# Shared experts, first half: two groups by seven block products, weight sums through GpSimd's queue, one routed matrix split in the routed stage

## The chip, the cores and the metric

One core of one Trainium2 chip runs the whole program. The metric is the device time of an execution in microseconds (us). Three runs of the kernel before took 1921.5 to 1924.93 us, with a median of 1923.02.

## The reference, cut to what matters

Four layers, each added to its input, work on `x` of 2 x 2048 tokens with 512 features, in single precision. The third is a mixture of experts, and the change lies in it:

```python
for e in range(2):                       # shared experts, hidden width 1024 each
    h = silu(x @ s_w1[e].T) * (x @ s_w3[e].T)
    shared_out += h @ s_w2[e].T
s = sigmoid(concat(x, t_emb) @ W_router.T)   # top 2 of 8 experts per token
for e in range(8):                       # routed experts, hidden width 512
    h = gelu(x @ r_w1[e].T)
    routed_out += h @ r_w2[e].T * gates[:, e:e+1]
out = (shared_out / 2 + routed_out) / 4
```

Before it stand a gate with a Haar-like transform and a recurrent layer, behind it a leaky recurrent layer.

## The kernel before, in words

**Stages in order of time.** Recurrent layer (to about 268 us), `shared_part` with `part` 0 for the first four groups of 512 tokens (269.9 to 788), `routed_part` for the routed experts (to about 1158), `shared_part` with `part` 1 for the other four groups (to about 1663), leaky layer (to the end).

**An item.** The two shared experts together have 16 tiles of 128 hidden columns (`HID`). One item `n` is one tile of one group of 512 tokens; `gl, i = divmod(n, HID)`, so a part has 64 items in four groups 0 to 3. Every factor is kept as two half-precision parts (high and low), and a product is three products of parts: high by high, low by high, high by low. A *plain* item is `first(n)` (line 1334: two banks of 12 products of 512 columns) and `second(n)` (line 1405: 12 products of 512 columns into four banks that run over the whole group). Between them ScalarE takes silu of the first bank (L1610), VectorE multiplies by the second (L2083), ScalarE casts the high half (L1581) and VectorE subtracts for the low half (L1990).

**A seven-product item.** The two halves of `first` form a 2 x 2 block product, which can be done with seven block products of 256 columns (L1344, 42 products) in place of eight, from sums and differences of blocks of the weights and of `x`. Three weight sums of a tile (`ring_pair`, `ring_one`) are read back from the tensor `mixed`, a fourth (`s3`) is put over a quarter of the tile in the arena. The sums of `x` are made on VectorE (`raw_block`) and split like `x` (`split_block`, `low_block`). TensorE does `first_four(n)`, `second(n-2)`, `last_three(n)`; in between VectorE adds the block products (`middle_sums`, `last_sums`), ScalarE copies one and takes silu in two halves. Before, part 1 uses this for groups 1 to 3 and part 0 not at all.

**Weight sums.** Part 0 makes them, for part 1, in the items behind `MIX_AT`: SyncE loads 512 KB of a weight tile into the one buffer `mix` (L1161), VectorE adds four times (`mix_sums`, L1926 to L1931), ScalarE casts the high half into `mixed` (`mix_high`, L1547; it waits for the store of the sum before), VectorE makes the low half (`mix_low`, L1935), and SyncE stores 512 KB (L1165). Five of the sixteen stand in items 15 to 23, every second one, eleven in items 41 to 61.

**What else stands in part 0's items.** Weight tiles are split up to item 13 (`split_tile`). From item 2 to 25 the router looks at the tokens: of every three items two split a look of 512 tokens (`split_look`, L1541 and L1843, four blocks a look at two per item) and turn it by transposing DMAs, the third has the logits on TensorE (L1419) and the store of the look. Then come the routing steps (`route`), the row sums of the routed weights on VectorE (`row_sums`, L1717, 16 items), and the splitting of the 16 routed matrices (`split_matrix`, L1528 and L1710), eleven of which lie in the arena over tiles of shared weights and wait in group 3 until these have been used (`h_used`). `leave` adds a finished group to its residual (L2195). The order on each engine's queue is written out by hand, item by item; each engine works its queue in order. GpSimd issues only the gathers of token rows (L2167, L2245) here.

```python
act.wait_ge(mix_sum, MIXES * (t + 1))          # mix_high, ScalarE
if t:
    act.wait_ge(mix_stored, 16 * t)
nc.scalar.activation(mixed[:, :, 0, :], mix[:].rearrange("p (s n) -> p s n", s=MIXES), ACT.Copy, scale=scl[:, 1:2]).then_inc(mix_hi, 1)
```

Of the kernel before, what the change touches and what calls it, by code (L numbers as in the profile page):

```python
# [14 lines left out]
P = 128  # L15
# [844 lines left out]
QUARTER = PIECE // 2  # L860
MIXES = 4
MIX_AT = tuple(range(14, 24, 2)) + tuple(range(40, 62, 2))
# [6 lines left out]
def matrix_end(b):  # L869

    last = RBASE + (b + 1) * 2 * MATRIX - 1
    return last // (2 * TILE) if last < EBASE else None

# [47 lines left out]
def shared_part(nc, src, part, keep, x_in, x_out, dram):  # L921
# [13 lines left out]
    LOADED = HID if first_part else HID - 1  # L935
    load_tile = lambda q: hidden(q + HID - LOADED)

    with ExitStack() as ctx:
# [11 lines left out]
        if first_part:  # L950
            mix, mixed = sb("mix", [P, MIXES * QUARTER]), sb("mixed", [P, MIXES, 2, QUARTER], F16)
        else:
            v1, u2, ring_pair1 = sb("v1", [P, CW]), sb("u2", [P, CW]), sb("ring_pair1", [P, 4 * QUARTER], F16)
# [26 lines left out]
        chain, hop = sem("chain"), sem("hop")  # L980
        if first_part:
# [30 lines left out]
            mix_in, mix_sum, mix_hi, mix_lo, mix_stored = (sem(n) for n in ("mix_in", "mix_sum", "mix_hi", "mix_lo", "mix_stored"))  # L1012
# [7 lines left out]
        else:  # L1020
# [8 lines left out]
            s_in, s3_in = [sem("s_in0"), sem("s_in1")], [sem("s3_in0"), sem("s3_in1")]  # L1029
            x_first, y_first, x_second, y_second = (sem(n) for n in ("x_first", "y_first", "x_second", "y_second"))  # L1030
            v1_ready, u2_ready, w_ready, c22_ready, c_ready, silu2_ready = (sem(n) for n in ("v1_ready", "u2_ready", "w_ready", "c22_ready", "c_ready", "silu2_ready"))
            t_raw, lo_ready, lo_stored, lo_back = (sem(n) for n in ("t_raw", "lo_ready", "lo_stored", "lo_back"))
# [18 lines left out]
        ROUTE_STEPS = 8 + LISTS + 1  # L1051
# [3 lines left out]
        ROUTE_AT = look_at(LOOKS)  # L1055
        NORM_AT = ROUTE_AT + 1
        SCALE_AT = NORM_AT + NORMS_R
        order = [b for b in range(2 * EXPERTS) if matrix_end(b) is None] + [b for b in range(2 * EXPERTS) if matrix_end(b) is not None]
        E_AT = SCALE_AT + 3

        def split_at(j):

            last = matrix_end(order[j])
            return E_AT + j if last is None else (PART_GROUPS - 1) * HID + (last - 1) + 1

# [14 lines left out]
        plain = lambda n: first_part or n < HID  # L1080
# [15 lines left out]

        if not first_part:
            halves = {"b11": (0, 0), "b21": (0, 1), "b12": (1, 0), "b22": (1, 1)}

            def quarter_of(x, name):  # L1100
                c, k = halves[name]
                return x[:, c, k * KD // 2:(k + 1) * KD // 2, :]

            raw_t = {n: xold[:, i // 2, i % 2 * KD // 2:(i % 2 + 1) * KD // 2, :] for i, n in enumerate(("t1", "t3", "t2", "t4"))}
            X_ORDER = ("b11", "b21", "b22", "t1", "t3", "t2", "t4")

            def x_block(gl, name):


                slot_x, high, low = xres[slot(gl)], xh[slot(gl)], xl[slot(gl)]  # L1110
                if name in halves:
                    return [quarter_of(t, name) for t in (slot_x, high, low)]
                if name == "t1":
                    return [raw_t[name], quarter_of(high, "b12"), quarter_of(low, "b12")]
                more = extra[gl % 2][:, ("t2", "t3", "t4").index(name)]
                return [raw_t[name], more[:, 0], more[:, 1]]
# [3 lines left out]
        with nc.Block(no_gpsimd_drain=True) as block:  # L1120
            @block.sync
            def _(sp):
# [35 lines left out]
                def load_mix(t):  # L1158
                    if t:
                        sp.wait_ge(mix_lo, t)  # L1160
# [151 lines left out]
            def _(pe):  # L1312
# [185 lines left out]
                if not first_part:  # L1498
                    second(ITEMS - 2)
# [974 lines left out]
```

## Time and profile before

| | us |
|---|---|
| median of three runs | 1923.02 |
| the profiled execution | 1924.83 |
| its span, first to last instruction | 1923.2 |
| TensorE busy in the span | 1889.9 (98%) |
| VectorE / ScalarE / GpSimd busy | 1161.6 / 913.6 / 157.2 |
| `shared_part`, part 0 | 269.9 to 788 |

Rows of a timeline give the start in us from the span's start, the duration (of a merged run of like instructions), the engine (PE is TensorE's products, DVE VectorE, ACT ScalarE, POOL GpSimd, SPq SyncE's DMA issues), the line, what is written and read, and in brackets the idle time of the engine just before with what ended it. The duration of a product is its latency; products overlap, so a rate is read from starts.

### The profile page before, as it was taken

The numbers are of one execution on the slowest core, as the hardware profiler recorded it, in microseconds if no ns is written. First come the engines' busy times: TensorE is split into PE (matmuls) and PEld (weight loads), VectorE is DVE, ScalarE is ACT, GpSimd is POOL, SyncE is SP. The second block draws the span as 40 slices with busy tenths as digits, with TensorE's granted clock in tenths as the row PEclk, the third lists the DMA queues.
The fourth block names the chain that finished last, engine by engine and source line by source line (L and its number), as shares of the span: only waits on it lengthen the run. The fifth ranks groups of instructions, "written<-read, shape, count | busy, mean of one in ns | idle before, by whom it ended". The sixth has DMA issues, their size and how long they took to land. (4 is left out here: it accounts for less than half of the span.)

```text
span 1923.2 us, 46865 instructions
## 1 busy us (share of the span) xinstructions
PE 1889.9 (98%) x18676; PEld 1220.0 (63%) x18676; DVE 1161.6 (60%) x2541; ACT 913.6 (48%) x1939; POOL 157.2 (8%) x159
## 2 busy tenths in 40 slices
PE   8999989999999999999999999999999999999998
PEld 7999954444444434444444444457777777799997
DVE  6666646555688565412111115678877887688887
ACT  4444445424122344434333335534445554488886
POOL 0000000000000000122121102111111120000000
PEclk8999999999999999999999999999999999999999
DMA  7033337876453565799999967655554467233223
GB/s 309 14 131 131 132 139 190 228 210 196 144 176 121 197 201 182 166 258 204 225 217 198 208 142 240 188 165 167 147 169 138 138 163 245 75 112 90 47 47 58
DMA packets 307486, 312.94 MB, mean 163 GB/s; under 512 B 229416, under 2 KB 248494, under 8 KB 300399
## 3 DMA queue, kind: packets, MB, share of 16 engines
q1 hardware_dynamic: 294334, 267.01, 48.2%
q0 software_dynamic: 12960, 43.26, 9.6%
q8 instruction: 134, 2.20, 0.5%
q14 instruction: 58, 0.47, 0.1%
HBM read 190.93 MB, written 73.14 MB: 137 GB/s over the span
## 5 line engine op out<-in xcount | busy, mean ns | idle before, releaser
L1334 PE MATMUL sh_p<-xh,arena 128*128 128x512 f16 x1280 | 383.5, 381 | 7.4 <-ACT sh_gated L1610 4.8
L1405 PE MATMUL p<-sh_h_hi,arena 128*128 128x512 f16 x1024 | 304.6, 379 | 1.0 <-DVE sh_h_lo L1990 1.0
L1334 PE MATMUL sh_p<-xl,arena 128*128 128x512 f16 x640 | 244.1, 381 | 0.0
L2351 DVE SCALAR_TENSOR_TENSOR ro_hs<-ro_h,fac,ro_hs 128x512 f16<-128x512 f32 x71 | 53.4, 752 | 295.2 <-ACT ro_hs L2337 290.8
L1334 PEld LDWEIGHTS sh_p<-xh,arena 128*128 128x128 f16 x1280 | 125.7, 98 | 160.6 <-issue 5.9
L2294 PE MATMUL ro_py<-arena,ro_ht 128*128 x852 | 195.0, 379 | 0.0
L1405 PE MATMUL p<-sh_h_lo,arena 128*128 128x512 f16 x512 | 194.0, 379 | 0.0
L1581 ACT CAST sh_h_hi<-sh_gated 128x512 f16<-128x512 f32 x128 | 79.1, 618 | 234.4 <-DVE sh_gated L2083 207.7
L1405 PEld LDWEIGHTS p<-sh_h_hi,arena 128*128 128x128 f16 x1024 | 96.4, 98 | 106.7 <-DVE sh_h_lo L1990 1.7
L2294 PEld LDWEIGHTS ro_py<-arena,ro_ht 128*128 128x128 f16 x852 | 83.4, 98 | 100.5 <-issue 0.2
L2083 DVE SCALAR_TENSOR_TENSOR sh_gated<-sh_p,fac,sh_gated 128x512 f32<-128x512 f32 x80 | 59.9, 749 | 101.9 <-PE sh_p L1334 101.6
L1344 PE MATMUL sh_p<-xh,arena 128*128 128x256 f16 x672 | 118.1, 273 | 0.8 <-DVE sh_u L1969 0.4
L1990 DVE TENSOR_TENSOR sh_h_lo<-sh_gated,sh_h_hi 128x512 f16<-128x512 f32 x128 | 88.1, 688 | 47.5 <-ACT sh_h_hi L1581 47.2
L2333 ACT ACTIVATE ro_h<-ro_pf,fac 128x512 f32<-128x512 f32 x71 | 48.8, 687 | 137.0 <-PE ro_pf L2294 137.0
L1610 ACT ACTIVATE sh_gated<-sh_p,fac 128x512 f32<-128x512 f32 x80 | 54.5, 682 | 120.8 <-PE sh_p L1334 120.7
L1334 PEld LDWEIGHTS sh_p<-xl,arena 128*128 128x128 f16 x640 | 62.9, 98 | 76.5 <-issue 1.6
L2181 POOL DMA_INDIRECT arena<-routed_rows,slots x64 | 72.9, 1139 | 355.0 <-DVE sh_pair L1839 344.5
L381 PE MATMUL rnn_acc<-rnn_x_hi,rnn_wx_hi 128*128 128x256 f32 x336 | 98.9, 309 | 1.8 <-ACT rnn_wx_hi L510 1.8
L2294 PE MATMUL ro_pf<-arena,xres 128*128 x432 | 99.0, 379 | 1.3 <-PEq L1120 1.3
L551 ACT ACTIVATE rnn_h_hi<-rnn_acc,rnn_inv_scale 128x256 f16<-128x256 f32 x84 | 39.8, 474 | 125.2 <-PE rnn_acc L398 125.2
L1344 PE MATMUL sh_p<-arena 128*128 128x256 f16 x720 | 98.2, 273 | 0.6 <-DMA arena<-mixed 0.6
L381 PE MATMUL leaky_acc<-leaky_x_hi,leaky_wx_hi 128*128 128x256 f16 x352 | 96.1, 273 | 0.5 <-DVEq L680 0.5
(335 smaller groups left out, 3960.5 us busy)
## 6 DMA issues: line engine op xcount, KB each, us to landing
stage<-in_shared_w SPq DMA_DIRECT2D x29, 768.0 KB, 5.3
routed_rows<-xres SPq DMA_DIRECT2D x71, 256.0 KB, 2.6
stage<-in_norms_r SPq DMA_DIRECT2D x16, 1024.0 KB, 4.9
stage<-in_routed_w SPq DMA_DIRECT2D x16, 1024.0 KB, 6.4
stage<-in_norms SPq DMA_DIRECT2D x14, 1024.0 KB, 5.0
arena<-x SPq DMA_DIRECT2D x12, 1024.0 KB, 5.7
x<-xres SPq DMA_DIRECT2D x16, 512.0 KB, 2.6
x_rows<-arena SPq DMA_DIRECT2D x8, 1024.0 KB, 9.0
```

Source lines behind the costliest of these rows:

```text
L381: mm = nc.tensor.matmul(acc[p][:, m, :], w[:, k, cols], x[p][:, k, :], start=(not gate and by_ones(q) and m % 2 == 0 and k == 0 and x is x ...
L1334: mm = nc.tensor.matmul(p1[u % P1][:], arena[:, w:w + P], x[slot(gl)][:, :, k, :], start=(j == 0), stop=(j == 3 * KD - 1))
L1344: mm = nc.tensor.matmul(out, a, b, start=(start and k == 0 and a is w_hi and b is x_hi), stop=(k == KD // 2 - 1 and b is x_lo), skip_group ...
L1405: mm = nc.tensor.matmul(p2[m][:], arena[:, w:w + P], h[n % 2][:], start=(i == 0 and j == 0), stop=(i == HID - 1 and j == 2))
L1581: nc.scalar.copy(h_hi[n % 2][:], full_h[n % 2] if plain(n) else gated[:, 0:GW]).then_inc(hh_ready, 1)
L1610: nc.scalar.activation(sig[n % 2], p1[2 * n % P1][:], ACT.Silu, scale=fac[:, 0:1]).then_inc(silu_ready, 1)
L1990: nc.vector.tensor_tensor(h_lo[n % 2][:], full_h[n % 2] if plain(n) else gated[:, 0:GW], h_hi[n % 2][:], ALU.subtract).then_inc(h_ready, 1)
L2083: nc.vector.scalar_tensor_tensor(full_h[n % 2], p1[(2 * n + 1) % P1][:], fac[:, 6:7], sig[n % 2], ALU.mult, ALU.mult).then_inc(full_ready, 1)
L2181: nc.gpsimd.indirect_dma_start(y[number % 2], None, dram["y"], bass.IndirectOffsetOnAxis(ap=slots[:, c, t:t + 1], axis=0)).then_inc(y_in[n ...
L2294: mm = nc.tensor.matmul(out, a[:, lhs + k * P:lhs + (k + 1) * P], experts[:, bass.ds(e, 1), w0 + w + k * D:w0 + w + (k + 1) * D].rearrange ...
L2333: nc.scalar.activation(h[t % 2], pf[t % 2][:], ACT.Gelu, scale=fac[:, 2:3]).then_inc(g_done, 1)
L2351: nc.vector.scalar_tensor_tensor(hs[t % TURNS][:, D:2 * D], h[t % 2], fac[:, 3:4], hs[t % TURNS][:, 0:D], ALU.mult, ALU.subtract).then_inc ...
```

## The change

- Groups 2 and 3 of part 0 are done in seven-product items (`SEVEN` is the first such item: 32 in part 0, 16 in part 1). The code for it, part 1's before, is shared by both parts; the blocks of `x` for group 2 are made in items 23 to 30, for group 3 in items 39 to 46.
- All sixteen weight sums stand in items 12 to 27, one in each. Two buffers `mix` are loaded, one `mixed` is kept. GpSimd's queue issues loads and stores, the loads of `s3`, and in groups 2 and 3 the ring loads. The quarter of tile 0 that `s3` covers is stored at item 15 and brought back in the routed stage.
- Row sums of the routed weights go from VectorE's reduction to four activations with an accumulated output on ScalarE. The lists of routed rows take three VectorE operations an item where there were sixteen. `route` starts one item later and has one empty step.
- Fifteen of the routed matrices are split in group 3 (before: eleven there, five in items just ahead of and behind its start), the one with number 10 at the start of the routed stage. The two matrices of an expert change places.
- Three token rows are gathered ahead of the routed stage where there were four.

```diff
-MIX_AT = tuple(range(14, 24, 2)) + tuple(range(40, 62, 2))
+MIX_AT = tuple(range(11, 11 + HID))
+MATRIX_AT = {15: 0, 11: 1, 12: 2, 13: 5, 14: 9}
+LATE_MATRIX = 10
...
+    SEVEN = 2 * HID if first_part else HID
...
-        plain = lambda n: first_part or n < HID
+        plain = lambda n: n < SEVEN
...
-            mix, mixed = sb("mix", [P, MIXES * QUARTER]), sb("mixed", [P, MIXES, 2, QUARTER], F16)
+            mix = [sb("mix", [P, MIXES * QUARTER])[:], keep["spare"][:].bitcast(F32)]
+            mixed = sb("mixed", [P, MIXES, 2, QUARTER], F16)
...
-                    if first_part and n in MIX_AT:
-                        load_mix(MIX_AT.index(n))
+                    if first_part and n == KEPT_AT:
+                        sp.wait_ge(stage_done, LOADED)
+                        sp.dma_start(dram["a21"], mixed_place(arena, 0)).then_inc(kept_out, 16)
...
+                def row_sums(b):
+                    q = LOADED + b
+                    act.wait_ge(stage_in[q % 2], in_stage(q))
+                    if b == 0:
+                        act.wait_ge(stage_done, LOADED)
+                    for r in range(KD):
+                        part = stage[q % 2][:, r * D:(r + 1) * D]
+                        total = nc.scalar.activation(part, part, ACT.Abs, accum_out=keep["sums"][:, NORMS_S + b, r:r + 1])
+                    total.then_inc(stage_done, 1)
...
                     act.wait_ge(mix_sum, MIXES * (t + 1))
                     if t:
                         act.wait_ge(mix_stored, 16 * t)
-                    nc.scalar.activation(mixed[:, :, 0, :], mix[:].rearrange("p (s n) -> p s n", s=MIXES), ACT.Copy, scale=scl[:, 1:2]).then_inc(mix_hi, 1)
+                    nc.scalar.activation(mixed[:, :, 0, :], mix[t % 2].rearrange("p (s n) -> p s n", s=MIXES), ACT.Copy, scale=scl[:, 1:2]).then_inc(mix_hi, 1)
...
+                    elif r == 0:
+                        dve.wait_ge(x_loaded[slot(gl)], 16 * ((gl + 1) // 2))
+                        dve.wait_ge(xt_stored, 16 * LOOKS)
...
-                    if i == (0 if first_part else 1) and gl:
+                    if i == (0 if gl < SEVEN_GROUP else 1) and gl:
                         leave(gl - 1)
...
+                    def load_mix(t):
+                        if t >= 2:
+                            pool.wait_ge(mix_lo, t - 1)
+                        pool.dma_start(mix[t % 2], src["shared_w"][hidden(t)][:, 0:2 * PIECE]).then_inc(mix_in[t % 2], 16)
+
+                    def store_mix(t):
+                        pool.wait_ge(mix_lo, t + 1)
+                        pool.dma_start(dram["mixed"][hidden(t)], mixed_flat).then_inc(mix_stored, 16)
+
+                    def load_s3(i):
+                        pool.wait_ge(p1_filled, 2 * (SEVEN - HID + i) + 2)
+                        pool.wait_ge(mix_stored, 16 * (i + 1))
+                        if hidden(i) == 0:
+                            pool.wait_ge(kept_out, 16)
+                        pool.dma_start(mixed_place(arena, hidden(i)), dram["mixed"][hidden(i)][:, 4 * QUARTER:6 * QUARTER].rearrange("p (h n) -> p h n", h=2)
+                                       ).then_inc(s3_in[i // (HID // 2)], 16)
+
+                    def load_mixed(n):
+                        e, t = n - SEVEN, hidden(n % HID)
+                        if e >= 2:
+                            pool.wait_ge(y_second, e - 1)
+                        pool.dma_start(ring_pair[e % 2], dram["mixed"][t][:, 0:4 * QUARTER]).then_inc(s_in[e % 2], 16)
+                        pool.dma_start(ring_one[e % 2], dram["mixed"][t][:, 6 * QUARTER:8 * QUARTER]).then_inc(s_in[e % 2], 16)
+
+                    pool.wait_ge(p1_filled, 2 * MIX_AT[0])
+                    load_mix(0)
+                    load_mix(1)
+                    for t in range(HID):
+                        store_mix(t)
+                        if t + 2 < HID:
+                            load_mix(t + 2)
+                        if t >= S3_AFTER:
+                            load_s3(t - S3_AFTER)
...
-                for t in range(RING, SLOT_TILES):
-                    pool.wait_ge(xt_in[t % XT], 16 * ((t - RING) // XT + 1))
+                for t in range(RING - 1, SLOT_TILES):
+                    if t >= RING:
+                        pool.wait_ge(xt_in[t % XT], 16 * ((t - RING) // XT + 1))
...
+                act.wait_ge(*late_loaded)
+                for a in (late_at + MATRIX // 2, late_at):
+                    nc.scalar.activation(arena[:, a:a + MATRIX // 2], late_raw[:, a - late_at:a - late_at + MATRIX // 2], ACT.Copy, scale=scl[:, 5:6]).then_inc(late_hi, 1)
...
+                for half, a in enumerate((late_at + MATRIX // 2, late_at)):
+                    dve.wait_ge(late_hi, half + 1)
+                    nc.vector.scalar_tensor_tensor(arena[:, MATRIX + a:MATRIX + a + MATRIX // 2], late_raw[:, a - late_at:a - late_at + MATRIX // 2], scl[:, 5:6],
+                                                   arena[:, a:a + MATRIX // 2], ALU.mult, ALU.subtract).then_inc(late_lo, 1)
                 add_shared(nc, keep, 0, (PART_GROUPS - 1) % 2)
```

## Rows read from the trace of the kernel before

**Rows 1.** TensorE in order of time, group 0: start us, us, engine, line
```profile
297.48 0.59 PE L1405 MATMUL p<-sh_h_hi,arena 128*128 128x512 f16 x2
...
306.05 0.59 PE L1405 MATMUL p<-sh_h_hi,arena 128*128 128x512 f16 x2
...
313.82 0.59 PE L1405 MATMUL p<-sh_h_hi,arena 128*128 128x512 f16 x2
```

**Rows 2.** the same view, two seven-product items of the second half
```profile
1334.28 0.59 PE L1405 MATMUL p<-sh_h_hi,arena 128*128 128x512 f16 x2
...
1341.45 0.59 PE L1405 MATMUL p<-sh_h_hi,arena 128*128 128x512 f16 x2
```

**Rows 3.** order of time around 699 us, and one stretch's busy times
```profile
693.87 0.43 DVE L1926 TENSOR_TENSOR sh_mix<-sh_mix 128x256 f32<-128x256 f32 x1 [5.86 <-DMA sh_mix<-in_shared_w]
...
699.43 1.04 PE L1334 MATMUL sh_p<-xh,arena 128*128 128x512 f16 x2 [4.79 <-ACT sh_gated L1610]
...
core 0: us, PE busy (x) PEld busy (x) DVE busy (x) ACT busy (x) POOL busy (x), PEclk, DMA share, GB/s
...
697.00:703.60 6.60, 4.17 (x10) 1.50 (x11) 5.03 (x5) 3.59 (x5) 0.00 (x0) 0.50 0.20 71
```

**Rows 4.** order of time on VectorE and ScalarE, one weight sum in item 15
```profile
394.20 0.75 DVE L2083 SCALAR_TENSOR_TENSOR sh_gated<-sh_p,fac,sh_gated 128x512 f32<-128x512 f32 x1 [4.30 <-PE sh_p L1334]
...
396.24 0.42 DVE L1926 TENSOR_TENSOR sh_mix<-sh_mix 128x256 f32<-128x256 f32 x1
...
397.95 1.15 ACT L1547 ACTIVATE sh_mixed<-sh_mix,scl 128x1024 f16<-128x1024 f32 x1 [2.35 <-DVE sh_mix L1931]
...
401.07 1.28 DVE L1935 SCALAR_TENSOR_TENSOR sh_mixed<-sh_mix,scl,sh_mixed 128x1024 f16<-128x1024 f32 x1
```

**Rows 5.** DMA issues (count, KB each, median us to landing), and GpSimd's start
```profile
mixed<-sh_mixed SPq DMA_DIRECT2D x5, 512.0 KB, 6.7
...
mixed<-sh_mixed SPq DMA_DIRECT2D x11, 512.0 KB, 3.0
...
out<-leaky_hist POOLq DMA_DIRECT2D x15, 512.0 KB, 5.5
...
1323.73 0.69 DVE L1839 TENSOR_TENSOR sh_pair<-arena,sh_pair 128x512 f16<-128x512 f32 x1 [1.03 <-ACT sh_pair L1649]
...
1324.69 1.75 POOL L2181 DMA_INDIRECT arena<-routed_rows,slots  x1 [14.69 <-DVE sh_pair L1839]
```

**Rows 6.** busy times by stretch (columns as in rows 3): look stage, second half
```profile
380.00:475.00 95.00, 95.00 (x555) 44.76 (x553) 50.15 (x82) 33.52 (x50) 0.00 (x0) 1.00 0.71 208
...
1278.00:1380.00 102.00, 100.65 (x745) 72.06 (x744) 85.30 (x158) 40.95 (x77) 14.80 (x14) 1.00 0.50 148
```

**Rows 7.** order of time on VectorE, and ScalarE's groups from 380 to 475
```profile
785.83 2.48 DVE L1710 SCALAR_TENSOR_TENSOR arena<-stage,scl,arena 128x1024 f16<-128x1024 f32 x2 [1.64 <-ACT arena L1528]
...
L1541 ACT ACTIVATE arena<-arena,scl 128x512 f16<-128x512 f32 x16 | 10.6, 710 | 2.1 <-DMA arena<-x 2.1
...
1339.44 0.68 DVE L1983 TENSOR_TENSOR sh_gated<-sh_p,sh_u 128x512 f32<-128x512 f32 x1
...
1342.91 0.68 DVE L1990 TENSOR_TENSOR sh_h_lo<-sh_gated,sh_h_hi 128x512 f16<-128x512 f32 x1
```

**Rows 8.** order of time on TensorE, second half; who waited for whom there
```profile
1280.82 0.59 PE L1405 MATMUL p<-sh_h_hi,arena 128*128 128x512 f16 x2
...
1319.93 0.59 PE L1405 MATMUL p<-sh_h_hi,arena 128*128 128x512 f16 x2
...
PE p L1405 <- DVE sh_h_lo L1990: 1.0, 1, 1.0
```

**Rows 9.** order of time at the start of the routed stage
```profile
789.29 0.95 POOL L2245 DMA_INDIRECT xh<-x_rows,token_of  x1 [132.71 <-POOLq L1120]
...
789.54 5.35 PE L2294 MATMUL ro_pf<-arena,xres 128*128 x24 [1.33 <-PEq L1120]
...
793.40 1.23 SPq L2254 DMA_TRANSPOSE xres<-xh  x1
```

More of the change, by code:

```diff
@@ L1054, in shared_part @@
         look_at = lambda a: 2 + 3 * a
-        ROUTE_AT = look_at(LOOKS)
+        ROUTE_AT = look_at(LOOKS) + 1
         NORM_AT = ROUTE_AT + 1
         SCALE_AT = NORM_AT + NORMS_R
-        order = [b for b in range(2 * EXPERTS) if matrix_end(b) is None] + [b for b in range(2 * EXPERTS) if matrix_end(b) is not None]
-        E_AT = SCALE_AT + 3
+        matrix_at = {b: (PART_GROUPS - 1) * HID + (MATRIX_AT[b] if matrix_end(b) is None else matrix_end(b) + (1 if matrix_end(b) < HID - 2 else 2)) for b in range(2 * EXPERTS)}
+        order = sorted(matrix_at, key=lambda b: matrix_at[b])
+        assert order[-1] == LATE_MATRIX and SCALE_AT + 3 < matrix_at[order[0]]
         def split_at(j):
-            last = matrix_end(order[j])
-            return E_AT + j if last is None else (PART_GROUPS - 1) * HID + (last - 1) + 1
+            return matrix_at[order[j]]
         def stage_load(q):
@@ L1257, in _ @@
                         load_x(1)
-                    if i == (1 if first_part else 2) and gl:
+                    if i == (1 if gl < SEVEN_GROUP else 2) and gl:
                         store_x(gl - 1)
@@ L1495, in _ @@
                         last_three(n)
-                    elif n and (first_part or n < HID - 1):
+                    elif n and n < SEVEN - 1:
                         second(n - 1)
-                if not first_part:
-                    second(ITEMS - 2)
+                second(ITEMS - 2)
                 second(ITEMS - 1)
@@ L1622, in _ @@
                         split_tile(n + AHEAD)
[L1623 removed]
+                    if i in BLOCK_AT and in_sevens(gl + 1):
                         split_block(gl + 1, BLOCK_AT.index(i))
@@ L2106, in _ @@
                         mix_sums(MIX_AT.index(n - 1))
-                    if not first_part and gl + 1 < PART_GROUPS:
+                    if in_sevens(gl + 1):
                         for r in range(len(RAW_AT)):
@@ L2168, in _ @@
                                                      ).then_inc(keep["rows_in"][t], 16)
+                    for n in range((PART_GROUPS - 1) * HID + 2, ITEMS):
+                        load_mixed(n)
                     keep["spent"] = spent
+                    late = LOADED + NORMS_R + 2 * EXPERTS - 1
+                    keep["late_raw"] = stage[late % 2], (stage_in[late % 2], in_stage(late))
                 else:
@@ L2234, in routed_part @@
         rows_in = keep["rows_in"]
+        late_raw, late_loaded = keep["late_raw"]
+        used.append(late_loaded[0])
+        late_at = RBASE + LATE_MATRIX * 2 * MATRIX
+        late_hi, late_lo, kept_in = sem("late_hi"), sem("late_lo"), sem("kept_in")
+        assert LATE_MATRIX % 2 == 0 and late_raw is keep["stage"][1]
         stage_in, x_loaded, xh_ready, xl_ready = sem("stage_in"), sem("x_loaded"), sem("xh_ready"), sem("xl_ready")
```

250 lines of the change are left out of this document (143 added, 107 removed).

## The prediction, made before the change was run

> **What bounds the kernel now.** The busy times by engine put TensorE at 98% of the span, so the question of every stage is whether TensorE gets less to do and whether it is then still fed. I read four views. First, TensorE's order of time in the plain items [rows 1]: the second product of an item begins every 7.77 us (306.05 to 313.82), and 8.57 us where the router's logits lie between (297.48 to 306.05, so 0.80 for them). Second, the same in the seven-product items of the other half [rows 2]: 7.18 us apart. Third, the one place in the first half where TensorE starves [rows 3]: at 693.87 VectorE had waited 5.86 us for the 512 KB load of a weight sum, and behind the cast of that sum in ScalarE's queue the activation that frees TensorE's bank came late: 4.79 us idle at 699.43. From 697.0 to 703.6 the granted clock is 0.50, the 1.2 GHz level, at which 4.2 us of products (699.43 to 703.6) do the work of 2.1. So this stall costs 4.8 + 2.1 = 6.9 us. Fourth, the chain of one weight sum inside an item [rows 4], which decides what follows.
>
> **What the change takes away.** 32 items (groups 2 and 3) go from 7.77 to 7.18: 32 x 0.59 = 19.1 us, all on TensorE and so on the path. The sums leave group 3, and with them the load that was late: 6.9 us. Together 26.0.
>
> **Part 1: sixteen weight sums in sixteen consecutive items (12 to 27).** Before they stood in every second item. Per item the chain on VectorE is: gate product, wait for ScalarE's high half, low half, 2.04 us (394.20 to 396.24); four sums, 1.71 (to 397.95); then ScalarE's cast of the sum, two blocks of the router's look on both engines, and the low cast, 4.40 (397.95 to 402.35) [rows 4]. That is 8.15 us in an item with look blocks. In the one item of three that has the logits instead, the two casts alone stand there, 1.15 + 1.28 = 2.43, so 6.2. Three items: 22.5 of VectorE's time against 3 x 7.77 + 0.80 = 24.1 of TensorE's. It fits, with 1.6 us to spare. Some lateness is allowed: VectorE has an item's low half 2.1 us after the item's first products, and TensorE uses it after the second product of the item before and the first products of the next, 7.77 us after them, so 5.6 us of room. Items 12 and 13, which still split a weight tile, use about half of that up.
>
> There is a second loop, which the spacing of two items hid before: `mixed` is one buffer, and ScalarE's cast of sum t waits (`mix_stored`) until the store of sum t-1 has landed. So from one low cast to the next there pass GpSimd's start, the landing L, and 4.40 (or 2.43). GpSimd starts an issue 0.27 us after VectorE's end (1323.73 + 0.69 to 1324.69) [rows 5]. Three items: 3 x (0.27 + L) + 2 x 4.40 + 2.43 = 3 L + 12.0, equal to TensorE's 24.1 at L = 4.0. Each us of L above that costs 3 us in three items, so 14 in items 12 to 25, less some 2 us of the lateness still allowed. The queue behind the wait is ScalarE's whole item: look blocks, the next activation, the next high half; TensorE waits for the last two.
>
> L is not in the trace. Bounds: 3.0, SyncE's 512 KB store of the same buffer in the quieter items after 580; and 6.7, the same store in items 14 to 23 [rows 5], where it queued behind SyncE's own 1 MB look loads. GpSimd's only direct store of 512 KB lands in 5.5 [rows 5], in a stretch with little else, but it adds into memory (`accum_op` at line 302), which this one does not. The engines are 71% busy in the stretch (380 to 475) [rows 6], and seven more sums there add 1 MB each to its 19.8 MB. I take L = 4.5, between SyncE's quiet store and GpSimd's adding one: 14 x 0.5 - 2 = 5 us, and 1 more for item 16, whose four residual additions stand in the same queue, and item 26, where the first raw block waits for the last look's store. **6 us**; ends 0 (L up to 4.1) and 14 x 2.7 - 2 = 36.
>
> The Trainium skill, page "DMA: Bandwidth & Descriptors", section "Anatomy of one DMA — SWDGE (gpsimd) path", gives a DMA of GpSimd's queue as 2.0 us plus its bytes over 436e3, so 3.2 for 512 KB. By that the store loop never closes and this part costs nothing; by the rows above it costs 6.
>
> **Part 2: the seven-product groups.** TensorE waits per item for VectorE's three middle sums. In the other half these groups ran with VectorE busy 85.3 of 102 us and TensorE 100.65 [rows 6]. From the last sums to the low half is 4.15 us (1339.44 to 1343.59), one routed matrix adds 2.48 [rows 7]: 6.6 of 7.18 in group 3. The matrices that lie over shared weights wait for `h_used`, 5.2 us into the item, so VectorE ends some 1.7 us into the next; the middle sums have 2.3 us of room there, and the next matrix waits for `h_used` anyway, so it doesn't add up. At the group's second item the residual additions (four, 2.7 us) come on top: 1 us, ends 0 and 2. Entry: in the other half the first five items took 39.1 us (1280.82 to 1319.93) for 35.9 [rows 8], 3.2 too long; part of that is that half's own work, so 2, ends 0 and 4. Exit: the last low half comes 1.0 us late there [rows 8], and the first half has the same tail: 1.0. The pair of ring loads moves to GpSimd's queue; issued when an item ends, they have 7.8 us, and the landings in rows 5 are below that: 0.
>
> **Part 3: row sums on ScalarE.** Four activations per item for VectorE's reduction, items 28 to 43. Not shown with an accumulator; the plain one of that size is 0.71 [rows 7], so 2.8 per item. ScalarE was busy 41 of 102 us, 2.9 per item, in the other half [rows 6]: 5.7 of 7.18, hidden by TensorE: 0. At twice the price 8.6, 1.4 too much in twelve items: 17 at the upper end. Nothing below zero, since VectorE's reductions were hidden.
>
> **Part 4: the routed stage's start.** One row gather moves behind the barrier. Before, the gather issued at 789.29 let SyncE start its transpose at 793.40 [rows 9], 4.1 later; a transposed tile is used about as long again after that, so at 797.5 or a little more. The fourth tile's product was due after three others of 2.67 (5.35 for two, from 789.54), at 797.5: 0.6, ends 0 and 3. The late matrix (2.2 on ScalarE, 2.48 on VectorE) goes before the first residual additions and is covered by the first four products, 10.7 us: 0.
>
> **The sum.** -26.0 + 6 + 1 + 2 + 1 + 0.6 = -15.4. The profiled execution is 1924.83 outside and 1923.2 inside; it lies 1.8 above the median. 1923.0 - 15.4 = 1907.6, about 1908.
>
> **Rivals.** *The store lands early (L up to 4).* Part 1 costs 0 to 1. For it: SyncE's 3.0. Against: GpSimd's 5.5. Time 1901 to 1903. This is also what the skill's fit would give.
> *The store loop rules (slower).* Place: ScalarE's cast in items 12 to 25. Price: 14 us per us of L. It takes back the whole remaining 21.4 at L = 5.7 and turns slower (by 0.2%, 3.8 us) at L = 5.9; at 6.4 it costs 32 and the time is 1933. For it: 6.7 in this very stretch and 5.5 on this very queue. Against: the 6.7 contains a wait in SyncE's queue that GpSimd's does not have. A clock drop like that of rows 3 would add to it.
> *ScalarE is the bound in items 32 to 43* (row sums at twice the price): 1908 + 17 = 1925, no change.
> *The change doesn't do what it says*: if TensorE is not the bound in groups 2 and 3, items stay at 7.77 and 19 us are missing: 1927. Rows 6 speak against it.
>
> **How the numbers follow.** A measurement of this kernel can tell 0.2%, 3.8 us, from no change. Chances: forecast (L 4.1 to 5.3) 0.45; early store 0.24; store loop with L above 5.6 0.18; ScalarE or seven-product groups bound 0.13. Faster: the first two, and 0.04 from milder forms of the others, 0.73. Same: 0.12, where gains and stalls cancel. Slower: 0.15. Range: 1900 (early store and a free entry) to 1925 (L = 5.7); what is left out is the slower end and a little below. The likeliest case alone has 1902 to 1917.
>
> **What would show it.** Right: 7.18 us between second products in groups 2 and 3; no idle of TensorE by ScalarE near item 60; in items 14 to 25 short stalls by the activation or the low half, ScalarE's cast idle "by DMA mixed". The store's median landing is the number to read. Wrong: stalls in group 3 by the matrix's cast or by ring loads, TensorE waiting in items 28 to 43 for ScalarE, or a long first gap in the routed stage.

## The result, and the profile after

The change made the kernel slightly slower: 1927.26 us (median of 20 runs, 1921.99 to 1934.37) against 1923.11 (median of 20, 1921.5 to 1926.49), a ratio of 1.0021 with a 95% interval of 1.0015 to 1.0027. Forecast were 1908 and faster; the range ended at 1925. The profiled execution is the longest of the twenty (1934.37, span 1932.6), 7 us above the median, so its stalls are larger than those of a usual execution.

The table cuts the span at starts that the traces show: second(11) and second(29) are the first products on the second weights of items 11 and 29 (what is ahead of second(11) differs by some 1 us), then come the first and the last routed product. Each row is one profiled execution.

| kernel | second(11) to second(29) | to the first routed product | routed stage |
|---|---|---|---|
| before | 145.7 | 274.1 | 368.0 |
| forecast for after | 151.7 | 252.1 | 368.6 |
| after | 167.0 | 254.5 | 375.3 |

The middle column came nearly as forecast. The groups by seven products run at 7.18 us an item, as in [rows 2], and where group 3 had stalled [rows 3] it no longer does. TensorE in order of time, after, two items of group 3, those between which the old stall lay:

```profile
705.08 0.59 PE L1429 MATMUL p<-sh_h_hi,arena 128*128 128x512 f16 x2
...
712.26 0.59 PE L1429 MATMUL p<-sh_h_hi,arena 128*128 128x512 f16 x2
```

The loss is in the other two columns. First the items of the weight sums. Who waited for whom in items 11 to 30 (us in total, times, longest):

```profile
ACT sh_mixed L1580 <- DMA mixed<-sh_mixed: 47.9, 12, 7.3
...
PE sh_px L1443 <- DVE arena L1874: 16.7, 5, 5.9
...
PE p L1429 <- DVE sh_h_lo L2025: 0.3, 1, 0.3
```

TensorE waits 16.7 us in five places, all at the router's logits (L1443) and all for the low blocks of a look, and next to nothing for activations or low halves. The order of time on all engines over two sums, after, shows where the lateness comes from:

```profile
416.71 0.37 SPq L1219 DMA_DIRECT2D x_rows<-arena  x1
...
420.07 0.54 POOL L2204 DMA_DIRECT2D mixed<-sh_mixed  x1 [10.15 <-DVE sh_mixed L1966]
...
426.79 1.15 ACT L1580 ACTIVATE sh_mixed<-spare,scl 128x1024 f16<-128x1024 f32 x1 [5.70 <-DMA mixed<-sh_mixed]
...
431.49 0.56 POOL L2204 DMA_DIRECT2D mixed<-sh_mixed  x1 [9.65 <-DVE sh_mixed L1966]
...
436.32 1.15 ACT L1580 ACTIVATE sh_mixed<-sh_mix,scl 128x1024 f16<-128x1024 f32 x1 [3.81 <-DMA mixed<-sh_mixed]
437.37 1.32 ACT L1574 ACTIVATE arena<-arena,scl 128x512 f16<-128x512 f32 x2
438.11 1.41 DVE L1874 SCALAR_TENSOR_TENSOR arena<-arena,scl 128x512 f16<-128x512 f32 x2 [3.29 <-ACT arena L1574]
...
439.58 1.02 PE L1443 MATMUL sh_px<-router_both,arena 128*128 128x16 f16 x32 [5.93 <-DVE arena L1874]
...
441.01 0.56 POOL L2204 DMA_DIRECT2D mixed<-sh_mixed  x1 [7.73 <-DVE sh_mixed L1966]
```

A store goes out at 420.07, ScalarE's next cast can start at 426.79; the next pair is 431.49 and 436.32. The two look blocks stand behind that cast on both engines, and TensorE, which works its queue in order, stands at the logits meanwhile. In or right behind three of the five stalls (4.2, 5.9 and 3.3 us) the granted clock falls to 0.50, the 1.2 GHz level; at the two shorter ones (2.3 and 1.0 us) it does not. Busy times by stretch, after (the first three rows are these places, the fourth is the routed start, the last covers the sums):

```profile
core 0: us, PE busy (x) PEld busy (x) DVE busy (x) ACT busy (x) POOL busy (x), PEclk, DMA share, GB/s
436.00:442.80 6.80, 3.22 (x38) 1.74 (x39) 4.01 (x6) 3.56 (x5) 1.79 (x3) 0.50 0.65 165
405.30:412.10 6.80, 4.67 (x42) 2.19 (x42) 3.96 (x5) 2.43 (x5) 1.06 (x2) 0.50 0.78 191
...
494.00:497.50 3.50, 3.50 (x31) 1.57 (x29) 2.78 (x6) 1.24 (x2) 1.79 (x3) 0.51 0.85 91
...
801.20:808.10 6.90, 5.46 (x13) 2.02 (x14) 0.00 (x0) 0.12 (x1) 2.83 (x3) 0.51 1.07 234
...
379.00:519.00 140.00, 125.61 (x699) 57.55 (x700) 82.25 (x141) 50.54 (x68) 23.44 (x40) 0.94 0.88 250
```

So of the 21.4 us that this stretch grew (second(11) at 368.71 and second(29) at 535.73, for 369.81 and 515.46), 17.0 are waits. The other 4.4 are products at the 1.2 GHz level, less some 0.9 us of the routing's products that moved out of the stretch: the 4.67, 3.22 and 3.50 us of products in the first three rows do the work of half that.

Second, the start of the routed stage, after, in order of time:

```profile
790.64 2.03 POOL L2339 DMA_INDIRECT xl<-x_rows,token_of  x1 [22.08 <-issue]
...
795.58 1.24 SPq L2350 DMA_TRANSPOSE stage<-xl  x1
...
802.64 5.30 PE L2393 MATMUL ro_pf<-arena,stage 128*128 x12 [4.49 <-DMA stage<-xl]
```

Row 3's gather, now behind the barrier, lets its transpose go out at 795.58, where the kernel before could issue that of row 4 at 793.40 [rows 9]. The product on the transposed tile starts 7.1 us later, TensorE idles 4.49 before it and then runs at 1.2 GHz (the fourth row above): the stage is 7.3 us longer than before, where 0.6 was forecast. There is no other wait of TensorE in it.

### The profile page after: what moved, and what is told of

It is laid out like the page before. It is cut to its first block and busy times, and to the rows that moved or that the text cites. A ratio compares the mean times of both kernels' runs of the same rounds, so it can differ in the third digit from the quotient of the medians.

```text
span 1932.6 us, 48465 instructions
## 1 busy us (share of the span) xinstructions
PE 1878.6 (97%) x19252; PEld 1276.1 (66%) x19252; DVE 1186.3 (61%) x2563; ACT 975.4 (50%) x2137; POOL 220.4 (11%) x271
## 5 line engine op out<-in xcount | busy, mean ns | idle before, releaser
L1358 PE MATMUL sh_p<-xh,arena 128*128 128x512 f16 x768 | 229.6, 381 | 2.6 <-PEq L2331 1.6
L1368 PE MATMUL sh_p<-xh,arena 128*128 128x256 f16 x928 | 163.5, 273 | 2.0 <-DVE arena L2004 0.7
L1614 ACT CAST sh_h_hi<-sh_gated 128x512 f16<-128x512 f32 x128 | 79.1, 618 | 157.0 <-DVE sh_gated L2118 112.8
L1358 PE MATMUL sh_p<-xl,arena 128*128 128x512 f16 x384 | 146.0, 380 | 0.0
L1358 PEld LDWEIGHTS sh_p<-xh,arena 128*128 128x128 f16 x768 | 75.2, 98 | 94.2 <-issue 4.1
L1368 PE MATMUL sh_p<-xl,arena 128*128 128x256 f16 x464 | 126.5, 273 | 0.0
L1368 PE MATMUL sh_p<-arena 128*128 128x256 f16 x912 | 124.4, 273 | 0.4 <-DMA arena<-mixed 0.4
L1608 ACT ACTIVATE sh_gated<-sh_gated,fac 128x256 f32<-128x256 f32 x80 | 40.6, 508 | 156.9 <-DVE sh_gated L2018 156.9
L1368 PEld LDWEIGHTS sh_p<-xh,arena 128*128 128x128 f16 x928 | 90.0, 98 | 32.2 <-DVE sh_u L2004 1.9
L2393 PE MATMUL ro_pf<-arena,stage 128*128 x420 | 98.9, 386 | 4.5 <-DMA stage<-xl 4.5
```

What stands on the lines that cost most here:

```text
L1358: mm = nc.tensor.matmul(p1[u % P1][:], arena[:, w:w + P], x[slot(gl)][:, :, k, :], start=(j == 0), stop=(j == 3 * KD - 1))
L1368: mm = nc.tensor.matmul(out, a, b, start=(start and k == 0 and a is w_hi and b is x_hi), stop=(k == KD // 2 - 1 and b is x_lo), skip_group ...
L1608: nc.scalar.activation(gated[:, CW:2 * CW], gated[:, CW:2 * CW], ACT.Silu, scale=fac[:, 0:1]).then_inc(silu2_ready, 1)
L1614: nc.scalar.copy(h_hi[n % 2][:], full_h[n % 2] if plain(n) else gated[:, 0:GW]).then_inc(hh_ready, 1)
L2393: mm = nc.tensor.matmul(out, a[:, lhs + k * P:lhs + (k + 1) * P], experts[:, bass.ds(e, 1), w0 + w + k * D:w0 + w + (k + 1) * D].rearrange ...
```

## The experiments

The theories: A, the look's blocks come late to the logits, where TensorE has no room for lateness; B, the store loop itself is too slow for one sum an item; C, VectorE's and ScalarE's own work is too long; D, there are more transfers than the engines can carry. All runs are timed beside the same kernel before; ratios are to it. The table gives the three stretches of each profiled execution. These are single executions of kernels whose times scatter by several us (the change's by 12), so small differences between them show nothing.

| run | median us | ratio (95%) | second(11) to (29) | to routed | routed |
|---|---|---|---|---|---|
| e1 | 1913.1 | 0.9945 (0.9932 to 0.9958) | 154.4 | 253.4 | 371.9 |
| e2 | 1939.0 | 1.0078 (1.0065 to 1.0091) | 174.1 | 255.6 | 372.5 |
| e3, e3b | 1917.5 | 0.9966 (0.9954 to 0.9978) | 154.6 | 253.9 | 370.3 |
| e4 | 1928.1 | 1.0019 (1.0010 to 1.0027) | 162.7 | 253.5 | 374.8 |
| e5 | 1921.3 | 0.9987 (0.9978 to 0.9997) | 157.0 | 253.7 | 372.3 |
| e6 | 1933.9 | 1.0048 (1.0034 to 1.0062) | 167.8 | 256.4 | 376.1 |
| e7 | 1924.7 | 1.0004 (0.9995 to 1.0013) | 164.3 | 253.6 | 372.5 |
| e9 | 1927.5 | 1.0018 (1.0009 to 1.0027) | 163.8 | 254.8 | 371.8 |
| e10 | 1939.9 | 1.0073 (1.0059 to 1.0087) | 163.7 | 273.9 | 368.2 |
| e11 | 1919.2 | 0.9981 (0.9965 to 0.9997) | | | |
| e12 | 1919.4 | 0.9979 (0.9971 to 0.9988) | 146.2 | 267.5 | 369.4 |
| e13 | 1910.2 | 0.9927 (0.9914 to 0.9940) | 148.3 | 253.9 | 369.0 |
| e14 | 1909.0 | 0.9927 (0.9914 to 0.9940) | 149.8 | 253.3 | 369.1 |
| e15 | 1913.2 | 0.9940 (0.9923 to 0.9957) | 152.8 | 254.1 | 368.0 |

### What stalls the logits: e1, e2, e3

The edits, in short:

```
e1, ScalarE's item:
-  mix_high(...)                  ahead of split_look
+  mix_high(...)                  behind split_look
e2, TensorE's item:
-  first(n); logits(a); second(n - 1)
+  first(n); second(n - 1); logits(a)     (scores one item later)
e3, buffers:
-  act.wait_ge(mix_stored, 16 * t)
+  act.wait_ge(mix_stored[buf(t)], 16 * uses(t))   two buffers in turn
```

Expected of e1:

> Edit: in ScalarE's item the cast of the weight sum stands behind the two look blocks instead of ahead of them; nothing else. Theory A (the look blocks, queued behind a cast that waits for the store of the sum before, reach the logits late; TensorE takes the logits right after the item's first products, so there is no room): the waits of TensorE for the look's low blocks (16.7 us in five places in the profiled execution) and the 1.2 GHz stretches behind them go; 12 to 18 us below 1927, so 1909 to 1915. Theory B (the store loop is too slow for one sum an item, whatever stands behind it): the loop gets shorter too, by the look blocks, so also most of it. Theory C (VectorE's and ScalarE's work in these items is too long in itself, without any wait for the store): the work is the same, 1927, and the waits move to other operands.

Expected of e2:

> Edit: TensorE's logits stand behind the second product of the same item instead of ahead of it (about 2.6 us later, and no product of this item behind them), VectorE's reading of the scores and the last sigmoid one item later; the weight sums, their cast, the wait for the store and the order on ScalarE and VectorE are otherwise as in the changed kernel. Theory A: a look that is 2.6 us late costs nothing now and one that is 6 us late costs some 3, so at least 8 of the 17 us go, with the 1.2 GHz stretches: 1911 to 1918. Theory B: the lateness itself remains and grows from item to item; TensorE waits for the activation or the low half of the next items instead: 1923 to 1929.

Expected of e3:

> Edit: the split sums go into two buffers in turn (the second in the free part of the scratch), so the cast of sum t waits for the store of sum t-2; orders and transfers are as in the changed kernel. Theories A and B (the wait for the store is the source of the lateness): ScalarE's waits for the store (47.9 us in twelve places) go, and with them 12 to 18 us: 1909 to 1915. Theory C (the engines' own work is too long): 1925 to 1929. Theory D (the transfers of the sums crowd out the look's own transfers): 1925 to 1929, since the traffic is the same.

e1 gave 14 us, as forecast, and e3 10, some 2 short of its range, without any work taken away, so theory C falls, and D with it as a full account (the transfers were the same). The waits of e1 in items 11 to 30, where those of the change were 47.9 and 16.7:

```profile
ACT sh_mixed L1580 <- DMA mixed<-sh_mixed: 28.4, 10, 5.0
...
PE sh_px L1443 <- DVE arena L1874: 5.6, 5, 3.6
```

e2 went wrong for both theories: it became 12 us slower. Its waits in the same items:

```profile
ACT sh_mixed L1580 <- DMA mixed<-sh_mixed: 56.2, 12, 9.9
...
PE sh_px L1443 <- DVE arena L1874: 11.7, 5, 3.8
...
PE sh_p L1358 <- ACT sh_gated L1643: 6.2, 3, 4.4
```

With more room at the logits the waits there shrink from 16.7 to 11.7, but ScalarE's waits for the store grow, and TensorE now waits for its activation as well. So the room at the logits is not the cause; it is where the lateness comes due. Theory B fits the waits of all three: the store loop is too slow for its three items, and what TensorE does not wait for in one place it waits for in the next. It does not give e2's time (1923 to 1929 expected, 1939 measured): why e2 lost still more, 7 us in this stretch, is open. The logits also free the look's buffers later there; whether that is it was not tried.

The same kernel ran once more for its trace. Expected of e3b:

> The kernel with two buffers for the split sums once more, for its trace: where its 10 us over a free run went. If the wait for the store was all: no waits of ScalarE for the store and waits of TensorE at the logits below 3 us in all. If ScalarE's order is a cost of its own (the look behind a cast that waits for VectorE's sums): 5 to 8 us of waits at the logits remain, released by the look's low blocks. If the look's load is late, ScalarE's idle time names it (8 us once).

Who waited in items 11 to 30, e3b:

```profile
PE sh_px L1449 <- DVE arena L1880: 6.3, 3, 2.7
...
ACT arena L1580 <- DMA arena<-x: 2.9, 1, 2.9
```

With two buffers ScalarE's cast never waited for a store in these items; 6.3 us at the logits stayed, the second case of the text ahead: the look still stands behind a cast that waits for VectorE's sums. Once the look's own load was late, by 2.9.

### Is it the amount of traffic? e5, e9, e10

In these items the transfer engines were 88% busy (the last row of the busy times), so the amount itself was the next suspect.

```
e5, SyncE, on top of e1:
-  turn_look(a, k) x2; load_look(a + 1)
+  load_look(a + 1); turn_look(a, k) x2
e9, on the change alone:
-  pool.dma_start(mix[t % 2], src["shared_w"][hidden(t)][:, 0:2 * PIECE])
+  w = 2 * PIECE if t < 2 else QUARTER
+  pool.dma_start(mix[t % 2][:, 0:w], src["shared_w"][hidden(t)][:, 0:w])
e10, on the kernel before, GpSimd:
+  for n in ten items of 12 to 26: two loads of 512 KB into free scratch
```

Expected of e5:

> Edit: on top of the cast behind the look (1913), SyncE issues the load of the next look ahead of the four transposes of this one instead of behind them. In the kernel with the cast behind the look alone, ScalarE waited 8.9 us for the last look's load (issued at 462.98, behind transposes that took SyncE's queue 9.0 us for five), and the logits after it cost 13.69 and 10.06 us for two items of 8.57 and 7.77. If SyncE's order makes the load late: those 7 us go, 1905 to 1908. If the load is late because the transfer engines are full (the load itself 8.5 us): it lands late all the same, 1911 to 1914.

Expected of e9:

> Edit on the changed kernel (1927) alone: from the third weight sum on, GpSimd loads only a quarter of the raw columns (128 KB for 512); every instruction, order, wait and store stays, and the sums are of older columns (left out: three quarters of the raw values, so the weights of groups 2 and 3 are other numbers). Theory of the transfer engines (items 12 to 27 ask for 35 MB, which at the 250 to 276 GB/s seen takes 127 to 140 us, where TensorE needs 121; everything that waits for a transfer is late by turns): 5.5 MB less bring the stretch to 29.5 MB and some 110 us, the stores land near 4 us, the waits at the logits shrink below 6 us: 1911 to 1916. Theory of order (the look behind the cast and the store loop are too long by themselves): stores still land after 4.6 to 5.1, 1923 to 1927.

Expected of e10:

> Edit on the kernel before: twenty more loads of 512 KB on GpSimd's queue into free scratch, two in each of ten items between 12 and 26, that nothing uses and only VectorE's first routing step waits for, long after; 10.5 MB more in the stretch, near what the change moves there. Theory of the transfer engines: although no sum was added, the stretch gets longer; the look's load, its transposes and its stores are late and TensorE waits at the logits: 3 to 8 us slower, 1927 to 1932. Theory of order: traffic alone costs nothing, 1923 to 1925.

e9 left the time where it was (1927.5). The transfers shrank, from 32.2 MB to 28.8 in the same 130 us, the stalls hardly did. The DMA view of 380 to 510 us, e9 (the last row: count, KB each, median us from issue to landing):

```profile
DMA packets 26988, 28.79 MB, mean 221 GB/s; under 512 B 19849, under 2 KB 20105, under 8 KB 26725
...
mixed<-sh_mixed POOLq DMA_DIRECT2D x14, 512.0 KB, 4.0
```

And who waited in items 11 to 30, e9:

```profile
ACT sh_mixed L1580 <- DMA mixed<-sh_mixed: 45.4, 12, 7.1
...
PE sh_px L1443 <- DVE arena L1874: 13.6, 5, 5.7
```

The median landing is 4.0 us, yet ScalarE waits for stores almost as long as in the change (45.4 for 47.9), and TensorE 13.6 for 16.7. The median landing fell as the theory of the transfer engines had it; the time and the waits came out as the theory of order had them. The reason is in the single stores. From a store's issue to the next cast that waited for it, three in a row: after 6.7, 4.8, 4.2 and 6.3, 3.9, 4.5; e9 7.2, 4.2, 4.0 and 7.9, 3.9, 4.0. One in three is long, and in the change it is always the one issued within a few us of SyncE's 1 MB store of the look's rows (416.71 and 420.07 above; also 387.39 and 389.40, 448.96 and 447.94, 476.76 and 474.78). That this store is what holds it up is read from the times; a kernel without it was not tried.

e5 fits neither of its cases: it became 8 us slower than e1, 7 above the upper range. With the look's load ahead of the transposes, ScalarE waited once 9.8 us for the transposes that free the look's buffer, and for the sums' stores up to 7.9; a transfer that is moved up moves others back. The waits of e5 in the same items:

```profile
ACT sh_mixed L1580 <- DMA mixed<-sh_mixed: 40.7, 11, 7.9
...
ACT arena L1574 <- DMA arena<-arena: 9.8, 1, 9.8
```

e10 shows that traffic can stall this stretch too, but it is not clean, and at 1939.9 it is slower than either case had it: of its 13 us at the logits and routing, half follows from the wait that was added for the extra loads. Its waits in the same items:

```profile
DVE arena L1880 <- DMA arena<-in_shared_w: 11.7, 1, 11.7
...
PE sh_px L1422 <- DVE arena L1846: 6.5, 1, 6.5
PE sh_px L1480 <- DVE arena L1884: 6.4, 1, 6.4
```

The first wait is VectorE's for the extra loads, and the 6.4 at L1480 follow from it. The 6.5 at L1422 come from traffic, but through the order again. Order of time, e10:

```profile
450.62 0.42 DVE L1930 TENSOR_TENSOR sh_mix<-sh_mix 128x256 f32<-128x256 f32 x1 [2.62 <-DMA sh_mix<-in_shared_w]
...
452.33 1.15 ACT L1550 ACTIVATE sh_mixed<-sh_mix,scl 128x1024 f16<-128x1024 f32 x1 [5.06 <-DVE sh_mix L1935]
453.39 1.32 ACT L1544 ACTIVATE arena<-arena,scl 128x512 f16<-128x512 f32 x2
```

The load of a weight sum, issued at 440.49, landed after 10.1 us; its cast waited on ScalarE, and the look's blocks stood behind that cast, as in the old stall of [rows 3] the activation did.

### The start of the routed stage: e4, e6, e7

```
e4: group 3 keeps its two running sums elsewhere from item 6 of the group on
+  row 3 gathered in group 3, ahead of the barrier
e6, on top of e4:
+  pool.wait_ge(xt_in[3], 16)     ahead of the gather of row 4
e7, on top of e4, ScalarE and VectorE:
-  late matrix in halves of 1024 columns
+  the 512 columns under row 3's transposed tile first, then 1536
```

Expected of e4:

> Edit: the two running sums of group 3 move, from its seventh item on, out of the place of gathered row 3 into the free half of the other residual buffer, and row 3 is gathered in that group, ahead of the barrier, as in the kernel before. The split of the late matrix stays behind the barrier. If the late gather holds up the routed stage (its transpose issued at 795.5, with three other gathers in flight, and landed 7 us later): the 4.5 us idle of TensorE at 802.6 and the 1.2 GHz stretch go, 5 to 7 us: 1920 to 1922. If it is the late matrix (its split frees the place of the third and fourth transposed tile): at most 2 us, 1925 to 1927.

Expected of e6:

> Edit: on top of the early gather of row 3 (1928), GpSimd's gathers of rows 4 and later wait until the transpose of row 3 has landed. Theory of contention (in the profile the transpose of row 3 was issued while gathers were in flight and landed 7 to 8 us later, where two transposes alone took 3): row 3's tile is there about 3.5 us after its issue, the 1.9 us of idle at the fourth product go, row 4 comes later but in time; the routed stage starts 3 to 5 us sooner: 1923 to 1925. If the gathers are not what holds it, rows 4 to 6 come later for nothing: 1929 to 1932.

Expected of e7:

> Edit: on top of the early gather of row 3 (1928), the late matrix is split in two unequal pieces, the quarter that lies in the place of row 3's transposed tile first (512 columns), then the rest, so that this tile's transpose waits for 1.2 us of ScalarE and VectorE instead of 2.4 and goes out right behind that of row 2, ahead of the gathers, as in the kernel before. Theory: the wait of 1.3 us for the late matrix let the gathers of rows 4 and 5 overtake the transpose; without it the start is the one before, 5 to 6 us better: 1921 to 1923. If the gathers slow it anyway, or GpSimd's first gather (2.03 us instead of 0.95) does: 1926 to 1928.

e4 alone gave nothing (1928.1, above both of its ranges). Row 3 was there in time, but its transpose now waited 1.3 us for the late matrix, and it went out among the gathers of rows 4 to 6. Order of time, e4:

```profile
785.85 2.03 POOL L2350 DMA_INDIRECT xh<-x_rows,token_of  x1 [22.07 <-issue]
...
787.10 1.23 SPq L2361 DMA_TRANSPOSE stage<-xl  x1
...
795.23 2.76 PE L2404 MATMUL ro_pf<-arena,stage 128*128 x12 [1.88 <-DMA stage<-xl]
...
800.88 1.60 PE L2404 MATMUL ro_py<-arena,ro_ht 128*128 x4 [2.89 <-DMA ro_ht<-ro_hs]
```

Issued at 787.10, it landed 8.0 us later. The longer wait, 2.89, is for the first transposed tile of the second step: its transpose stands in SyncE's queue behind that of row 4, and the gather of row 4 took 9.0 us to land. With the last quarter first (e7) the fourth product had no idle, and the median fell by 3.4, between the two ranges, though its one profiled execution shows a later wait of 2.6 us for a transposed tile of the second step. Holding the gathers back (e6) did what its first case said to row 3's tile, which landed after 4.4 us instead of 8.0 and was not waited for, but it made row 4 late: TensorE waited 5.7 us for the first transposed tile of the second step, again behind the transpose of row 4, and the time rose to 1933.9. In the five profiles with e4 and e7 together (e7, e12 to e15) the stage is 368.0 to 372.5, four of them within 1.5 us of the kernel before; in the six with the change's start (after, e1, e2, e3b, e5, e9) 370.3 to 375.3. So the start costs some 4 us, up to 7.3. With row 3 early and the late matrix still behind the barrier it costs as much (e4), partly by a late gather; the late row alone was not tried, and the shares of the two are open.

### Putting it together: e11 to e15

```
e11 = e1 and  MIX_AT: items 12 to 29, without 18 and 24
e12 = e11 with e3, e4 and e7
e13 = e1, e3, e4, e7, sums in items 12 to 27 as in the change
e14 = e1, e4, e7 (one buffer), sums in items 12 to 27
e15 = e13 with sums in items 12 to 28, without 21
```

Expected of e11:

> Edit: the cast behind the look (1913) and the sixteen sums over eighteen items (12 to 29, none in 18 and 24) instead of sixteen. Theory of the transfer engines: 1 MB less in two of the windows of three items, so 2 to 5 us: 1908 to 1911. If only the order mattered: 1912 to 1914. Risk: the last sum ends two items later, and the first ring loads of group 2 come behind its store: up to 4 us back, seen as TensorE waiting for ring tiles at item 32.

Expected of e12:

> Edit: cast behind the look, sums over eighteen items, two buffers for the split sums, row 3 gathered early, and the late matrix's last quarter first. If the parts add up (cast 14, two buffers some of the 28 us that ScalarE still waits for stores, spread 2 to 5, start of the routed stage 3): 1902 to 1907. If the transfer engines set the stretch whatever the order: the two buffers add nothing, 1906 to 1910.

Expected of e13:

> Edit: cast behind the look, two buffers for the split sums, row 3 early and the last quarter first, the sums in sixteen items in a row again (12 to 27). With the sums over eighteen items this had no stall in items 12 to 27, but 11.7 us at item 32, where the first ring tiles came late (1919). If the order and the second buffer ended the stalls: 1919 less 11.7, so 1906 to 1909. If it was the thinner spread that ended them: stalls at the logits again, 1911 to 1915.

Expected of e14:

> Edit: cast behind the look, row 3 early, the last quarter first; one buffer and sixteen items in a row as in the change. The start of the routed stage gave 3 us in the comparison without the cast behind the look; if it adds up, 1913 less 3: 1909 to 1911. If the one buffer still stalls the logits by turns: 1912 to 1916, with ScalarE waiting for stores some 28 us.

Expected of e15:

> Edit: as the one without spread, but the sums over seventeen items (12 to 28, none in 21). The last store comes one item later. If the first ring tiles of group 2 still come in time: 1906 to 1909, equal to no spread; if they are late as with eighteen items, about half of the 11.7 us: 1911 to 1915.

e11 (1919.2) and e12 (1919.4) lie above all their ranges. e12 had no stall to speak of in items 12 to 27. Its busy times there (columns as above):

```profile
380.00:510.00 130.00, 129.47 (x714) 60.24 (x712) 86.59 (x151) 52.95 (x76) 21.11 (x36) 1.00 0.94 260
```

But it lost as much at item 32, as who waited for whom from 365 to 540 us shows:

```profile
PE sh_p L1378 <- DMA sh_mixed<-mixed: 8.1, 1, 8.1
```

TensorE is busy 129.5 of 130 us with the transfer engines at 94%: a stretch so full of transfers did not stall it. The last sum was stored two items later, the first ring tiles came behind it, and the step from second(29) to second(30), which holds the first products of items 31 and 32, took 23.65 us for the 11.98 of the runs without spread. e11 (whose trace is not used) has the same spread and the same time. One gap (e15) costs 0.6 there and gave nothing back; its 1913.2 lies in the second range, but not by the late ring tiles that this range was worked out from.

e13 and e14 are the best, 14 us below the kernel before, and equal within their intervals (e14 as forecast, e13 some 1 us above its better range). So the order of the cast is enough; the second buffer adds nothing that shows. The waits of e14 in items 11 to 30:

```profile
ACT sh_mixed L1584 <- DMA mixed<-sh_mixed: 35.9, 12, 5.5
...
PE sh_px L1447 <- DVE arena L1880: 3.1, 4, 1.7
```

ScalarE still waits 35.9 us for stores, and TensorE 3.1 for the looks: the wait has lost what stood behind it.

## Why the prediction was wrong

*The gains* were right: 7.18 us an item and no stall in group 3. *Part 2* (4 us with entry and exit) is right within 2.4 in the change and 1.2 to 4.3 in the runs that keep its items, the middle column against 252.1; some 0.9 us of the routing's own products also moved from the first column into this one. *Part 3* is right. ScalarE's groups from 530 to 660 us, after:

```profile
L1560 ACT ACTIVATE stage<-stage 128x512 f32<-128x512 f32 x60 | 36.9, 615 | 0.0
L1560 ACT ACTIVATION_READ_ACCUMULATOR stage<-stage 128x1 f32 x60 | 11.2, 186 | 0.0
```

Four such pairs are 3.2 us an item for the 2.8 assumed; TensorE did not wait for ScalarE in these items.

*Part 1, the first failed step: "I take L = 4.5"*, with 6 us as its price and "less some 2 us of the lateness still allowed". The loop was seen, with its place and its threshold, L = 4.0. It failed in the size of L, in the room, and in the place of the wait. The median landing came out as taken:

```profile
mixed<-sh_mixed POOLq DMA_DIRECT2D x16, 512.0 KB, 4.6
```

But the loop adds up every landing, and one in three is 5.9 to 6.7. Over the eleven stores of items 13 to 24 that ScalarE waited for, issue to cast is 5.1 on average (one more, in item 25, took 10.9, with no logits left behind it); the same formula at 5.1 gives 14 x 1.1 - 2 + 1 = 14, near the 17.0 of waits. The 6.7 of [rows 5] was set aside because SyncE's store had waited behind SyncE's own loads; GpSimd's stores in the same place took as long. By the fit in the Trainium skill, "DMA: Bandwidth & Descriptors", section "Anatomy of one DMA — SWDGE (gpsimd) path", the estimate for 512 KB is 3.2. The trace agrees where it is quiet: the two stores behind the last look, at 516.41 and 525.71, landed after 3.0; those between the looks took 3.7 to 10.8, and there the measurements decide. The 2 us of room did not exist at the logits (without it the formula gives 16). There the prediction had the wait wrong: "TensorE waits for the last two", the next activation and high half, but it waited 0.3 us for a low half and 16.7 for the look's blocks. And the clock, which the rival only mentioned, took the other 4.4 of the stretch.

The size of the fix follows from the same sum. Behind the look, cast to low cast is 2.46 us in every item, so three items need 3 L + 8.2: the threshold rises from 4.0 to 5.3, above the 5.1 that the stores took in the change. In e14 they took 5.6 (the ten in the same items that were waited for): 14 x 0.3 = 4, for the 3.1 that TensorE waited. The edit shortens the loop and takes the looks out from behind the wait at once; no run separates the two.

*Part 4, the second failed step: "0.6, ends 0 and 3".* It took the before's 4.1 us from gather to transpose and as much again to the product. The gather took 2.03 us on GpSimd instead of 0.95 and its transpose went out 4.9 us after its start; the transpose, now behind three more gathers, took 6.9 to land. The late matrix, put at 0, did not hold it in the change (split by 793.0, and the gather landed at 795.56); with row 3 early it holds the same transpose back by 1.3 (e4).

Of the rivals, the slower one came about (the store loop rules), at a smaller L than its 5.9, since the clock and the routed start paid part of the price. From 1907.6: 11 more of waits in Part 1, 4.4 more in the same stretch, by the clock, 6.7 in Part 4 and some 2 in the middle give 1932, the profiled execution's 1932.6 to 1934.4; the median is 7 lower.

## What to carry to other kernels

When an engine waits in its queue for a transfer, price the wait by the mean of its landings where they will stand, not by a quiet median, and list what stands behind it: here moving one cast behind two unrelated instructions was worth 14 us. Ask of a loop through a buffer what the other engines have inside it; taking their work out of it does as much as a second buffer. A gather moved past a barrier also brings what depends on it among whatever the barrier releases: here row 3's transpose, which landed after 6.9 us with three more gathers ahead of it, for 4.5 before.

## What the runs showed that was not expected

Less traffic did not shorten the waits (e9: 28.8 MB for 32.2), and with the transfer engines busy for 94% of a stretch TensorE ran almost without a stall (e12): here the order of the queues, and which transfers meet, counted for more than the amount. Two edits that give an operand earlier or later as intended (e5, e2) made the time worse by 8 and 12 us; in e5 a buffer came free later, in e2 the cause is open. At stalls of 4.2 and 5.9 us the granted clock fell to 0.50 for 6.8 us each, at one of 3.3 us for 3.4.
